# Score products of 32 rows in eight array tiles, and a second attention whose output has features on partitions

## The chip, the cores and the metric

One core of one Trainium2 chip runs the whole program. The metric is device time in microseconds (us) of one execution; lower is better. The core has a matrix engine (TensorE, PE in the profile, with its weight loads as PEld), three engines for elementwise work (VectorE as DVE, ScalarE as ACT, GpSimd as POOL) and a queue of transfers issued by SyncE (SP). Matrix products go to PSUM, a memory of eight banks of 512 fp32 columns on 128 partitions; everything else is in SBUF.

## The reference

The input `x` (128, 64, 384) and a mask `adj` (128, 64, 64) go through two attention layers. Every one of the 128 graphs has 64 nodes of 384 features.

```python
h = jnp.maximum(_layernorm(x), 0.0)
# layer 0, 12 heads of 32: additive scores
hv = einsum('bnd,ade->bane', h, W);  th = tanh(hv)
attn = leaky(src + swap(dst))            # src, dst: th times w_src, w_dst
attn = softmax(where(~adj, -999, attn))
feat = elu(attn @ hv + b);  gate = sigmoid(h @ H_w.T + H_b)
x = x + gate * feat + (1 - gate) * h
h = jnp.maximum(_layernorm(x), 0.0)
# layer 1, 6 heads of 64: q, k, v projections
probs = softmax(q @ k.T / 8 + where(adj, 0, -9e15))
x = x + (probs @ v).reshape(...) @ Wf + bf
```

## The kernel before

The tokens are cut into 16 groups of 512 (four tiles of 128 tokens, each tile two graphs of 64 nodes). The program of every engine is written out by hand as a sequence of passes `i = 0..16`: pass `i` does layer 0 of group `i` and layer 1 of group `j = i - 1`, so every pass but the first and the last holds both. Engines meet only through semaphores (`wait_ge`, `then_inc`). A table, `RING`, lists the PSUM banks in the order in which PE fills them; a job takes bank `place % 8`, and `take` makes PE wait until the job that used that bank eight places earlier has been read.

Products of the big weights are made in fp32r in three parts, high times high, low times high, high times low (`product`). For that ACT copies a transposed tile out of PSUM rounded to fp32r (the high part: `hT0h`, `hT1h`), and DVE subtracts it from the PSUM value (the low part: `hT0l`, `hT1l`). Everything else on PE is plain fp32; each such matmul of the program is two MATMUL records of the trace (a transpose is one).

PE's work in one pass, in order: the values of layer 0 and the gate (two times four products of nine matmuls), transposes of `th` and of the normalised layer-1 input (kept in `p1`), `wsd` products (source and destination scores), `project` for q and k with layer 0's score products `blocks` between them, `values1`, layer 1's scores, transposes of both layers' probabilities, `attend0` for four token tiles and `attend1` for two pairs of them, transposes of the next group's `h0` and of the second attention's output, and the last product with `Wf`.

`blocks(pair)` computes the additive scores of one pair of token tiles in eight matmuls of 32 rows, 64 output partitions and 384 columns: operands of token tile `t` stand on partitions 32t to 32t+31, results of graph `g` go to output partitions 64g to 64g+63. So each matmul uses one of eight tiles of 32 rows by 64 columns of the array, and a call uses four of them, each twice:

```python
for half_of in range(2):
    for t in (2 * pair, 2 * pair + 1):
        for g in range(2):
```

`attend1(pair)` has the transposed, not yet normalised probabilities as stationary operand and the values `V1` with a column of ones as moving operand; its output has tokens on partitions and the row sum as 65th column. DVE (`divide1`) takes the reciprocal of that column and multiplies, into `p1`; PE transposes `p1` again (12 transposes, the job `attn1_low`); ACT and DVE make the high and the low part for the product with `Wf`.

`V1` is filled from `v_tok` by four DMAs (`values1_spread`), `mask1` is the last operation on DVE before the division of the attention outputs, and `seeded banks` are banks into which ACT has written the gate's bias or the mask before PE adds to them (`put_bias`, `put_mask`); these are unchanged.

## Time and profile before

| | before |
|---|---|
| time, median of 3 runs | 1048.03 us (1046.15 to 1048.07) |
| profiled execution: its time, its span | 1046.33 us, 1044.4 us |
| PE busy | 968.0 us, 93% |
| DVE busy | 775.1 us, 74% |
| ACT busy | 630.1 us, 60% |
| POOL busy | 273.4 us, 26% |
| mean granted clock of TensorE | 0.982 |

The profile is one execution, recorded instruction by instruction. The page gives busy times and shares; the views of the trace give instructions in order of time (the timeline), what ended each wait, and the chain of work that ended last. All times are in us from the start of the span. The 1.9 us between span and time lie before the first and after the last instruction.

### The profile page before, as it was taken

What the parts mean: (1) busy time and instruction counts of PE and PEld (TensorE: products, weight loads), DVE (VectorE), ACT (ScalarE), POOL (GpSimd) and SP (SyncE); (2) the same over time, 40 slices, a digit from 0 to 9 for tenths busy, and PEclk for the clock granted to TensorE, in tenths of its full rate; (3) what the DMA queues carried; (4) which work ended last, traced back from release to release, by engine and by line L of the source; (5) the groups of instructions that cost most, each with busy time, mean ns of one, the idle gap of its engine ahead of it and who ended that gap; (6) DMA issues with size and microseconds to landing.
All of it is one profiled execution on the core that took longest, in us unless ns stands there. A gap on an engine that the chain in (4) does not pass through costs nothing.

```text
span 1044.4 us, 24816 instructions
## 1 busy us (share of the span) xinstructions
PE 968.0 (93%) x10037; PEld 840.1 (80%) x10037; DVE 775.1 (74%) x1456; ACT 630.1 (60%) x1242; POOL 273.4 (26%) x338
## 2 busy tenths in 40 slices
PE   6689999999999999999999999999999999999696
PEld 5487978889797888978788897878879788887575
DVE  4868877777787778868777886877788687877814
ACT  5657576484746757485675747567574755756332
POOL 2223150502415041240504124050421405032110
PEclk9699999999999999999999999999999999999987
DMA  8310151420415143041513405141240414121102
GB/s 233 51 24 11 32 93 32 91 33 32 62 33 93 32 81 44 16 78 33 93 32 74 49 4 92 32 93 32 68 48 11 94 32 93 33 49 23 23 31 62
DMA packets 183797, 56.61 MB, mean 54 GB/s; under 512 B 164994, under 2 KB 183684, under 8 KB 183684
## 3 DMA queue, kind: packets, MB, share of 16 engines
q1 hardware_dynamic: 183684, 55.02, 28.9%
q8 instruction: 81, 1.33, 0.5%
q14 instruction: 32, 0.26, 0.1%
HBM read 17.26 MB, written 12.58 MB: 29 GB/s over the span
## 4 chain that ended last, share of the span: by engine, by line
PE 53%; DVE 25%; issue 9%; ACT 6%; POOL 4%; DMA 1%; SPq 0%; DVEq 0%; ACTq 0%; POOLq 0%
PE ps L661 12%; PE ps L663 11%; PE ps L662 11%; PE ps L647 7%; PE ps L739 5%; PE ps L839 4%; DVE x L1001 4%; DVE ee L998 4%; DVE hT0l L907 3%; DVE hT1l L1096 3%; PE ps L857 3%; ACT p L440 2%; DVE p L1026 2%; DVE mx L1024 2%; PE ps L805 2%
## 5 line engine op out<-in xcount | busy, mean ns | idle before, releaser
L420 POOL TENSOR_TENSOR x_in<-x_in,ee 128x384 f32<-128x384 f32 x64 | 68.5, 1070 | 615.1 <-DVE ee L1004 615.1
L1060 DVE TENSOR_TENSOR hT1l<-ps,hT1h 128x512 fp32r<-128x512 f32 x48 | 30.4, 684 | 93.5 <-ACT hT1h L575 93.4
L647 PE MATMUL ps<-ident,p 128*128 128x128 f32 x576 | 80.4, 285 | 19.3 <-ACT p L440 10.7
L413 POOL TENSOR_TENSOR x_in<-x_in,h 128x384 f32<-128x384 f32 x64 | 85.1, 1359 | 16.4 <-DVE Wf_lo L932 16.4
L1037 DVE COPY_PREDICATED_SCALAR z<-not_adj,masked 128x768 f32 x64 | 69.6, 1087 | 26.3 <-ACT z L528 26.3
L647 PEld LDWEIGHTS ps<-ident,p 128*128 128x128 f32 x576 | 65.5, 145 | 28.1 <-issue 12.5
L661 PE MATMUL ps<-Wf_hi,hT1h 128*128 128x384 f32 x192 | 69.0, 359 | 10.4 <-DVE hT1l L1096 10.4
L491 ACT ACTIVATE ps<-hb_all 128x384 f32<-128x384 f32 x56 | 27.7, 495 | 79.6 <-DVE x_in L1049 79.6
L407 POOL TENSOR_TENSOR x_in<-x_in,bf_row 128x384 f32<-128x384 f32 x64 | 62.4, 1008 | 43.1 <-ACT p L440 43.1
L528 ACT ACTIVATE z<-ps 128x384 f32<-128x384 f32 x128 | 52.5, 498 | 30.9 <-PE ps L739 30.9
L661 PE MATMUL ps<-W_hi,hT0h 128*128 128x384 f32 x192 | 65.4, 341 | 3.5 <-DVE hT0l L907 3.5
L509 ACT ACTIVATE QT<-ps,bq_col 128x512 f32<-128x512 f32 x48 | 33.0, 687 | 58.1 <-PE ps L663 58.1
L1016 DVE TENSOR_TENSOR v_tok<-ps,bv_row 128x384 f32<-128x384 f32 x64 | 34.2, 553 | 44.9 <-PE ps L663 44.9
L891 DVE BATCH_NORM_STATS2 stats<-x_in 128x6 f32<-128x384 f32 x128 | 63.2, 543 | 5.4 <-DMA x_in<-in_x_dram 5.4
L661 PE MATMUL ps<-hT1h,Wq_hi 128*128 128x512 f32 x144 | 60.0, 416 | 6.6 <-DVE hT1l L1060 6.6
L663 PE MATMUL ps<-W_hi,hT0l 128*128 128x384 f32 x192 | 65.1, 339 | 0.0
L662 PE MATMUL ps<-W_lo,hT0h 128*128 128x384 f32 x192 | 65.1, 339 | 0.0
L663 PE MATMUL ps<-Wf_hi,hT1l 128*128 128x384 f32 x192 | 64.6, 336 | 0.0
L663 PE MATMUL ps<-Wv_hi,hT1l 128*128 128x384 f32 x192 | 64.5, 336 | 0.0
L663 PE MATMUL ps<-Hw_hi,hT0l 128*128 128x384 f32 x192 | 64.5, 336 | 0.0
L662 PE MATMUL ps<-Wf_lo,hT1h 128*128 128x384 f32 x192 | 64.5, 336 | 0.0
L661 PE MATMUL ps<-Hw_hi,hT0h 128*128 128x384 f32 x192 | 64.5, 336 | 0.0
(132 smaller groups left out, 2820.0 us busy)
## 6 DMA issues: line engine op xcount, KB each, us to landing
V<-v_tok SPq DMA_DIRECT2D x128, 192.0 KB, 4.9
x_in<-in_x_dram SPq DMA_DIRECT2D x16, 768.0 KB, 5.0
out_dram<-x_in SPq DMA_DIRECT2D x16, 768.0 KB, 3.5
x<-in_L_gnn_H_w_dram SPq DMA_DIRECT2D x1, 576.0 KB, 5.9
QT<-in_L_gnn_W_dram SPq DMA_DIRECT2D x3, 192.0 KB, 6.7
thT<-in_L_gnn_Wq_dram SPq DMA_DIRECT2D x1, 576.0 KB, 8.1
z<-in_L_gnn_Wk_dram SPq DMA_DIRECT2D x1, 576.0 KB, 8.6
z<-in_L_gnn_Wv_dram SPq DMA_DIRECT2D x1, 576.0 KB, 9.7
```

The source lines that it names most:

```text
L407: pool.tensor_tensor(x_in[:, j % 3, t], x_in[:, j % 3, t], bf_row[:], ALU.add).then_inc(x2_biased, 1)
L413: pool.tensor_tensor(x_in[:, i % 3, t], x_in[:, i % 3, t], h0[:, par, t], ALU.add).then_inc(x_plus_h, 1)
L420: pool.tensor_tensor(x_in[:, i % 3, t], x_in[:, i % 3, t], ee[:, t], ALU.subtract).then_inc(x2_made, 1)
L528: act.activation(z[:, t, half_of * D:(half_of + 1) * D], ps[:, job("leaky_made", 2 * t + half_of) % BANKS, 0:D], ACT.Prelu, alpha=SLOPE).t ...
L647: return pe.transpose(dst, src, ident[0:rows, 0:rows])
L661: pe.matmul(dst, left_h(c), right_h(c), start=(c == 0 and not begun), stop=False, skip_group_check=begun)
L662: pe.matmul(dst, left_h(c), right_l(c), start=False, stop=False, skip_group_check=begun)
L663: mm = pe.matmul(dst, left_l(c), right_h(c), start=False, stop=(c == C - 1 and not more), skip_group_check=begun)
L739: mm = pe.matmul(ps[64 * g:64 * g + 64, job("leaky_made", 2 * t + half_of) % BANKS, 0:D], src_rows[rows, g * N:(g + 1) * N], thT[rows].rea ...
L839: mm = pe.matmul(bank[g * N:(g + 1) * N, k], turned[:, at * P + g * N:at * P + (g + 1) * N], V0[:, g, :, t, k], start=True, stop=True, ski ...
L891: dve.bn_stats(stats[:, layer, t], src).then_inc((stats0, stats1)[layer], 1)
L1037: dve.copy_predicated(zt, not_adj[:, t].unsqueeze(1).broadcast_to((P, HEADS0, N)), masked0[:].unsqueeze(2).broadcast_to((P, HEADS0, N))).t ...
```

## The change

**Score products.** `blocks` is called with a half of the heads instead of a pair of token tiles. It covers all four token tiles, graph 0 first and then graph 1, so each call uses all eight array tiles once. `leaky`, the mask, the maximum, the subtraction and `exp0` follow: their units are (half of the heads, pair of token tiles), with as many elements as before.

**Second attention.** The probabilities are normalised in SBUF before they are transposed (`divide1(pair)`: a sum, a reciprocal and a multiplication over 768 elements per partition, two pairs). `attend1` has the values as stationary operand (64 keys x 64 features) and the transposed probabilities as moving operand (64 queries), so its output has features on partitions and is copied straight into `hT1h`/`hT1l`; the 12 transposes of the attention output and the column of ones are gone. Odd token tiles keep the heads of a pair swapped in `p1` (`p1_heads`), so one token tile's two heads come from both halves of the rows and go into one bank, and the other token tile's two heads use the other two of the four 64 x 64 array tiles. Four matmul records in a row use the same array tile. `V1` is filled by eight DMAs of half the size.

**Order.** Transposes are made and copied by token tile (four banks of 384 columns) instead of by chunk of 128 features (three banks of 512). `turn_h0` comes in two halves, `attend0(2)` and the first half of it now stand ahead of the transposes of layer 1's probabilities, `attend0(3)` stands ahead of `attend1`. `project` does all high-part products first and waits for the low parts after that. `attend1`'s second call takes banks that were used by the first two `h0_low` jobs, its first call banks of `attend0(1)` and `attend0(2)`.

```diff
+        def p1_pair(pair):
+            return p1[:, pair * P1_PAIR:(pair + 1) * P1_PAIR].rearrange("p (t x) -> p t x", t=2)[:, :, 0:D]
...
+        def p1_heads(pair, o):
+            pitch = P1_TILE + N if o == 0 else P1_TILE - N
+            at = pair * P1_PAIR + N * o
+            return p1[:, at:at + 2 * pitch].rearrange("p (t x) -> p t x", t=2)[:, :, 0:D]\
+                .rearrange("p t (k w) -> p t k w", w=P)[:, :, :, 0:N]
...
             + jobs("probs0T_copied", 0, probs0T_copied, 6)
-            + jobs("attn0_made", 0, attn0_made, 4)[0:2]
+            + jobs("attn0_made", 0, attn0_made, 4)[0:3]
+            + jobs("h0_low", NEXT, h0_low, 4)[0:2]
             + jobs("probs1T_copied", 1, probs1T_copied, 3)
-            + jobs("attn0_made", 0, attn0_made, 4)[2:3]
-            + jobs("attn1_made", 1, attn1_made, 4)
             + jobs("attn0_made", 0, attn0_made, 4)[3:4]
-            + jobs("h0_low", NEXT, h0_low, 3)
-            + jobs("attn1_low", 1, attn1_low, 3)
+            + jobs("attn1_low", 1, attn1_low, 4)
+            + jobs("h0_low", NEXT, h0_low, 4)[2:4]
             + jobs("out_made", 1, out_made, 4)
...
+                        for r in range(2):
+                            for b in range(2):
+                                sp.dma_start(V1[64 * r:64 * r + 64, g, b].rearrange("p q k e -> p (q k) e"),
+                                             v_tok[64 * g:64 * g + 64, 2 * b:2 * b + 2]
+                                             .rearrange("p q (k o e) -> p (q k) o e", o=2, e=E1)[:, :, r ^ b])\
...
+            def high_tile(to, name, t):
+                toks = slice(t * P, (t + 1) * P)
+                return act.activation(to[:, :, toks], ps[:, job(name, t) % BANKS, 0:D].rearrange("p (c m) -> p c m", m=P), ACT.Copy)
...
+                if real(i + 1):
+                    h0_parts(i + 1, range(0, 2))
                 if real(j):
                     for c in range(3):
                         act.wait_ge(probs1_turned, 3 * j + c + 1)
                         act.activation(KT[:, c], ps[:, job("probs1T_copied", c) % BANKS], ACT.Copy).then_inc(probs1T_copied, 1)
                 exp_elu(0)
                 exp_elu(1)
+                exp_elu(2)
...
-                    for c in range(C):
-                        act.wait_ge(attn1_turned, C * j + c + 1)
-                        act.activation(hT1h[:, c], ps[:, job("attn1_low", c) % BANKS], ACT.Copy).then_inc(attn1_high, 1)
+                    for t in range(TILES):
+                        act.wait_ge(attn1_full, 2 * j + t // 2 + 1)
+                        high_tile(hT1h, "attn1_low", t).then_inc(attn1_high, 1)
...
+            def turn_tokens(name, ready, done, src, i, g, tiles=range(TILES)):
+
+                for t in tiles:
+                    take(i, job(name, t))
+                    pe.wait_ge(ready, TILES * g + t + 1)
+                    for c in range(C):
+                        mm = turn(ps[:, job(name, t) % BANKS, c * P:(c + 1) * P], src(t, c))
                     mm.then_inc(done, 1)
...
+                    dst = ps[:, job(name, o) % BANKS]
+                    pe.wait_ge(h1_high, TILES * (j + 1))
+                    for c in range(C):
+                        pe.matmul(dst, wh[w][:, c, cols], hT1h[:, c], start=(c == 0), stop=False)
+                        pe.matmul(dst, wl[w][:, c, cols], hT1h[:, c], start=False, stop=False)
+                    pe.wait_ge(h1_low, TILES * (j + 1))
+                    for c in range(C):
+                        mm = pe.matmul(dst, wh[w][:, c, cols], hT1l[:, c], start=False, stop=(c == C - 1))
+                    mm.then_inc(full, 1)
...
-                def blocks(pair):
-                    take(i, job("leaky_made", 4 * pair + 3))
...
-                    for half_of in range(2):
-                        for t in (2 * pair, 2 * pair + 1):
...
                             rows = slice(SD * t, SD * t + SD)
-                            for g in range(2):
-                                mm = pe.matmul(ps[64 * g:64 * g + 64, job("leaky_made", 2 * t + half_of) % BANKS, 0:D],
...
+                def blocks(half_of):
+                    for t in range(TILES):
+                        take(i, job("leaky_made", 4 * half_of + t))
+                    for g in range(2):
+                        for t in range(TILES):
...
+                            mm = pe.matmul(ps[64 * g:64 * g + 64, job("leaky_made", 4 * half_of + t) % BANKS, 0:D],
+                                           src_rows[rows, g * N:(g + 1) * N],
+                                           thT[rows].rearrange("p c m -> p (c m)")[:, (2 * g + half_of) * D:(2 * g + half_of + 1) * D],
+                                           start=True, stop=True, skip_group_check=True)
...
-                        take(i, job("attn1_made", 2 * pair + o))
-                    for t in range(2):
-                        for k in range(PAIRS1):
...
+                    for k in range(PAIRS1):
+                        for b in range(2):
+                            t = 2 * pair + b
+                            q, at = divmod(t * PAIRS1 + k, 4)
                             for o in range(2):
-                                rows = slice(64 * o, 64 * o + 64)
-                                bank = ps[:, job("attn1_made", 2 * pair + o) % BANKS, 0:HEADS1 * (E1 + 1)]\
-                                    .rearrange("p (t k e) -> p t k e", t=2, e=E1 + 1)
+                                rows = slice(64 * (o ^ b), 64 * (o ^ b) + 64)
                                 for g in range(2):
-                                    mm = pe.matmul(bank[g * N:(g + 1) * N, t, k], KT[rows, q, at * P + g * N:at * P + (g + 1) * N],
-                                                   V1[rows, g, t + 2 * pair, k], start=True, stop=True, skip_group_check=True)
+                                    mm = pe.matmul(ps[64 * o:64 * o + 64, job("attn1_low", t) % BANKS, k * P + g * N:k * P + (g + 1) * N],
+                                                   V1[rows, g, b, pair, k], KT[rows, q, at * P + g * N:at * P + (g + 1) * N],
+                                                   start=True, stop=True, skip_group_check=True)
...
                 attend0(0)
                 attend0(1)
-                if real(j):
-                    turn_probs("probs1T_copied", probs1_made, probs1_turned, p1, PAIRS1, j, 3)
                 attend0(2)
+                if real(i + 1):
+                    turn_h0(i, i + 1, 1 - par, range(0, 2))
+                if real(j):
+                    turn_probs("probs1T_copied", probs1_divided, pair_of, probs1_turned, p1_tile, PAIRS1, j, 3)
+                attend0(3)
                 if real(j):
                     attend1(0)
                     attend1(1)
-                attend0(3)
                 if real(i + 1):
-                    turn_h0(i, i + 1, 1 - par)
-                if real(j):
-                    pe.wait_ge(attn1_made, TILES * (j + 1))
-                    turn_tokens("attn1_low", attn1_made, attn1_turned, lambda t, c: p1[:, t, c * P:(c + 1) * P], i, j)
+                    turn_h0(i, i + 1, 1 - par, range(2, 4))
+                if real(j):
...
+                        pe.wait_ge(attn1_low, TILES * j + t + 1)
...
-                        pair, o = divmod(q, 2)
-                        v = ps[:, job("attn1_made", q) % BANKS, 0:HEADS1 * (E1 + 1)].rearrange("p (t k e) -> p t k e", t=2, e=E1 + 1)
-                        sums = rs1[:, q].rearrange("p (t k) -> p t k", t=2)
-                        dve.wait_ge(attn1_full, 2 * j + pair + 1)
-                        dve.reciprocal(sums, v[:, :, :, E1]).then_inc(inv1_made, 1)
-                        dve.wait_ge(inv1_made, TILES * j + q + 1)
-                        dve.tensor_tensor(p1[:, 2 * pair:2 * pair + 2].rearrange("p t (k o e) -> p t k o e", o=2, e=E1)[:, :, :, o],
-                                          v[:, :, :, 0:E1], sums.unsqueeze(3).broadcast_to((P, 2, PAIRS1, E1)), ALU.mult)\
-                            .then_inc(attn1_made, 1)
+                        probs = p1_pair(pair).rearrange("p t (h m) -> p t h m", m=N)
+                        sums = rs1[:, 2 * pair:2 * pair + 2]
+                        dve.wait_ge(probs1_made, TILES * j + 2 * pair + 2)
+                        dve.tensor_reduce(sums, probs, AX_X, ALU.add).then_inc(sums1_made, 1)
+                        dve.wait_ge(sums1_made, 2 * j + pair + 1)
+                        dve.reciprocal(sums, sums).then_inc(inv1_made, 1)
+                        dve.wait_ge(inv1_made, 2 * j + pair + 1)
+                        dve.tensor_tensor(probs, probs, sums.unsqueeze(3).broadcast_to((P, 2, HEADS1, N)), ALU.mult)\
+                            .then_inc(probs1_divided, 1)
...
+                divide1(0)
+                divide1(1)
                 divide0(0)
                 divide0(1)
                 divide0(2)
-                if real(j):
-                    dve.wait_ge(probs1_turned, 3 * (j + 1))
-                for q in range(TILES):
-                    divide1(q)
-                if real(j):
-                    for c in range(C):
-                        dve.wait_ge(attn1_high, C * j + c + 1)
-                        dve.tensor_tensor(hT1l[:, c], ps[:, job("attn1_low", c) % BANKS], hT1h[:, c].bitcast(F32), ALU.subtract)\
-                            .then_inc(attn1_low, 1)
+                if real(i + 1):
+                    h0_lows(i + 1, range(0, 2))
+                if real(j):
+                    for t in range(TILES):
+                        dve.wait_ge(attn1_high, TILES * j + t + 1)
+                        low_tile(hT1l, hT1h, "attn1_low", t).then_inc(attn1_low, 1)
                 divide0(3)
                 if real(i + 1):
-                    h0_lows(i + 1)
+                    h0_lows(i + 1, range(2, 4))
```

PE, from layer 1's scores (`KT,QT`) on to the first matmuls of the `Wf` product; `ident` rows are transposes, of layer 0's probabilities `z`, of `p1` and of `h0`, `V,QT` and `V,thT` are `attend0`, `V,KT` is `attend1`. Before:

```order
L805 MATMUL ps<-KT,QT 64x64 x48
L647 MATMUL ps<-ident,z 128x128 x24
L839 MATMUL ps<-V,QT 64x66 x24
L647 MATMUL ps<-ident,p 128x128 x12
L839 MATMUL ps<-V,thT 64x66 x12
L857 MATMUL ps<-V,KT 64x65 x48
L839 MATMUL ps<-V,thT 64x66 x12
L647 MATMUL ps<-ident,h 128x128 x12
L647 MATMUL ps<-ident,p 128x128 x12
L661 MATMUL ps<-Wf_hi,hT1h 128x384
```

After:

```order
L828 MATMUL ps<-KT,QT 64x64 x48
L668 MATMUL ps<-ident,z 128x128 x24
L868 MATMUL ps<-V,QT 64x66 x24
L868 MATMUL ps<-V,thT 64x66 x12
L668 MATMUL ps<-ident,h 128x128 x6
L668 MATMUL ps<-ident,p 128x128 x12
L868 MATMUL ps<-V,thT 64x66 x12
L885 MATMUL ps<-KT,V 64x64 x48
L668 MATMUL ps<-ident,h 128x128 x6
L682 MATMUL ps<-Wf_hi,hT1h 128x384
```

`attend1` has moved behind `attend0(3)`, half of the `h` transposes have moved in front of those of `p`, and 12 of the 24 `p` transposes are gone.

DVE, from `mask1` on (`x` is `x1`, the output of `attend0`; `rs` are sums and reciprocals). Before:

```order
L1084 TENSOR_SCALAR mask<-adj_in 128x256
L977 RECIPROCAL rs<-ps 128x12
L979 TENSOR_TENSOR x<-ps,rs 128x384
L977 RECIPROCAL rs<-ps 128x12
L979 TENSOR_TENSOR x<-ps,rs 128x384
L977 RECIPROCAL rs<-ps 128x12
L979 TENSOR_TENSOR x<-ps,rs 128x384
L988 RECIPROCAL rs<-ps 128x6
L990 TENSOR_TENSOR p<-ps,rs 128x6x64
```

After:

```order
L1118 TENSOR_SCALAR mask<-adj_in 128x256
L1020 TENSOR_REDUCE rs<-p 128x12
L1022 RECIPROCAL rs<-rs 128x12
L1024 TENSOR_TENSOR p<-p,rs 128x2x384
L1020 TENSOR_REDUCE rs<-p 128x12
L1022 RECIPROCAL rs<-rs 128x12
L1024 TENSOR_TENSOR p<-p,rs 128x2x384
L1010 RECIPROCAL rs<-ps 128x12
L1012 TENSOR_TENSOR x<-ps,rs 128x384
L1010 RECIPROCAL rs<-ps 128x12
```

The division of layer 1 stood behind three divisions of `attend0`'s output and read PSUM; it now stands ahead of them and works on 768 elements in SBUF.

PE, the first product of `project` behind the `wsd` products, with the semaphores waited for. Before:

```order
L661 MATMUL ps<-hT1h,Wq_hi 128x512 [waits h1_low,gate_tanh]
L662 MATMUL ps<-hT1l,Wq_hi 128x512
L663 MATMUL ps<-hT1h,Wq_lo 128x512
L661 MATMUL ps<-hT1h,Wq_hi 128x512 [waits h1_low]
L662 MATMUL ps<-hT1l,Wq_hi 128x512
L663 MATMUL ps<-hT1h,Wq_lo 128x512
L661 MATMUL ps<-hT1h,Wq_hi 128x512 [waits h1_low]
```

After:

```order
L749 MATMUL ps<-hT1h,Wq_hi 128x512 [waits h1_high,thT_copied]
L750 MATMUL ps<-hT1h,Wq_lo 128x512
L749 MATMUL ps<-hT1h,Wq_hi 128x512
L750 MATMUL ps<-hT1h,Wq_lo 128x512
L749 MATMUL ps<-hT1h,Wq_hi 128x512
L750 MATMUL ps<-hT1h,Wq_lo 128x512
L753 MATMUL ps<-hT1l,Wq_hi 128x512 [waits h1_low]
L753 MATMUL ps<-hT1l,Wq_hi 128x512 x2
```

Each third matmul used the low part `hT1l`, chunk by chunk; now six matmuls use the high part alone, and the wait for the low part stands behind them.

## Rows read from the trace of the kernel before

**Rows 1.** The page: busy times, and granted clock of TensorE in 40 slices.

```profile
PE 968.0 (93%) x10037; PEld 840.1 (80%) x10037; DVE 775.1 (74%) x1456; ACT 630.1 (60%) x1242; POOL 273.4 (26%) x338
PEclk9699999999999999999999999999999999999987
```

**Rows 2.** DVE's `mask1`, one a pass: times, first and last start, form.

```profile
L1084 DVE TENSOR_SCALAR mask<-adj_in x16: 282/283/285, 52.3 to 967.8; 128x256 bf16<-128x256 uint8 x16
```

**Rows 3.** One pass by windows: length, busy time of each engine, PEclk, DMA.

```profile
538.00:599.20 61.20, 59.20 (x629) 51.79 (x626) 47.50 (x89) 38.96 (x77) 16.84 (x20) 1.00 0.35 53
```

**Rows 4.** Timeline of PE: start, length, line, count [idle before <-releaser].

```profile
570.40 0.86 PE L753 MATMUL ps<-thT,wsd 128*32 128x128 f32 x24 [0.62 <-ACT thT L569]
571.70 0.47 PE L661 MATMUL ps<-hT1h,Wq_hi 128*128 128x512 f32 x1 [0.44 <-DVE hT1l L1060]
576.07 1.52 PE L739 MATMUL ps<-thT,src_rows 32*64 32x384 f32 x16
577.52 0.51 PE L661 MATMUL ps<-hT1h,Wq_hi 128*128 128x512 f32 x1
...
602.62 1.74 PE L857 MATMUL ps<-V,KT 64*64 64x65 f32 x96
604.28 0.92 PE L839 MATMUL ps<-V,thT 128*64 128x66 f32 x24
605.13 1.53 PE L647 MATMUL ps<-ident,h 128*128 128x128 f32 x12
606.62 1.53 PE L647 MATMUL ps<-ident,p 128*128 128x128 f32 x12
608.84 0.42 PE L661 MATMUL ps<-Wf_hi,hT1h 128*128 128x384 f32 x1 [0.69 <-DVE hT1l L1096]
...
615.46 0.34 PE L661 MATMUL ps<-W_hi,hT0h 128*128 128x384 f32 x1
```

**Rows 5.** Timeline of PE inside the first `blocks` call, two narrow windows.

```profile
576.77 0.50 PE L739 MATMUL ps<-thT,src_rows 32*64 32x384 f32 x4
...
577.09 0.50 PE L739 MATMUL ps<-thT,src_rows 32*64 32x384 f32 x4
```

**Rows 6.** Timeline of DVE in the same pass.

```profile
579.83 0.95 DVE L1040 TENSOR_REDUCE mx<-z 128x12 f32<-128x768 f32 x1
580.82 0.96 DVE L1042 TENSOR_TENSOR z<-z,mx 128x768 f32<-128x768 f32 x1
581.69 1.09 DVE L1037 COPY_PREDICATED_SCALAR z<-not_adj,masked 128x768 f32 x1
...
599.43 0.23 DVE L977 RECIPROCAL rs<-ps 128x12 f32<-128x12 f32 x1
599.69 0.56 DVE L979 TENSOR_TENSOR x<-ps,rs 128x384 f32<-128x384 f32 x1
...
612.33 0.55 DVE L998 SCALAR_TENSOR_TENSOR ee<-ee,x 128x384 f32<-128x384 f32 x1
```

**Rows 7.** Timeline of ACT at the turn of a pass, and behind it.

```profile
566.02 2.51 ACT L440 ACTIVATE p<-x_in,shift,rstd 128x384 f32<-128x384 f32 x4 [0.21 <-POOL shift L389]
...
568.80 1.54 ACT L569 ACTIVATE thT<-ps 128x512 f32<-128x512 f32 x3
...
577.72 1.64 ACT L528 ACTIVATE z<-ps 128x384 f32<-128x384 f32 x4 [0.85 <-PE ps L739]
...
599.35 0.94 ACT L539 ACTIVATE p<-p 128x384 f32<-128x384 f32 x2
```

**Rows 8.** The chain that ended last, in order of time: start, length, what.

```profile
619.58 0.46 DVE x_in L1049
...
632.83 0.14 issue
```

**Rows 9.** Timeline of SP, the four DMAs that fill `V1`.

```profile
594.69 3.64 SPq L348 DMA_DIRECT2D V<-v_tok x4
```

**Rows 10.** The page on the same DMAs: count, KB each, median us to landing.

```profile
V<-v_tok SPq DMA_DIRECT2D x128, 192.0 KB, 4.9
```

198 lines of the change are left out of this document (95 added, 103 removed).

## The prediction

> **What bounds the kernel now.** I read the page first: PE is busy 93% of the span, DVE 74%, and TensorE's clock is granted in full in all slices but the first and the last [rows 1]. So I look at PE's own waits. `mask1` comes once a pass; from the first to the last of its 16 starts are 915.5 us, 61.0 us a pass [rows 2]. One undisturbed pass cut out as a window has PE busy for 59.20 of 61.20 us, DVE for 47.5, ACT for 39.0 [rows 3]: PE idles 2.0 us a pass. The timeline of PE says where: 0.62 us before the `wsd` products for ACT's copy, 0.44 us before `project` for DVE's low part, 0.69 us before the product with `Wf`, again for a low part [rows 4]. The rest are crumbs inside the `Wf` product: its 36 matmuls and their waits last from 608.84 to 615.46, 6.62 us [rows 4]. PE work that is removed therefore counts in full unless another engine's chain runs beside it. Two such chains lie near: DVE's from the divisions to the end of the pass, and ACT's at the turn of the pass, where `normalise1` waits only 0.21 us for POOL behind its own earlier work [rows 7].
>
> The profiled execution took 1046.33 us (span 1044.4 and 1.9 around it). The median of the runs shown is 1048.03, 1.7 more; the sum is made on 1046.33 and 1.7 is added. No change is told from about 0.2% (2 us) on.
>
> **Score products.** A call of `blocks` takes 1.45 us, from 576.07 to the next product at 577.52, for 16 records; there are two calls a pass [rows 4]. Inside it, records start in fours, and the fours are 0.32 us apart [rows 5]. Four record groups make 1.28 us, and 0.17 us are start and end of the call. 0.32 us is what 384 columns take at two clocks of 2.4 GHz each, so a group of four is four matmuls side by side in four array tiles, and an array tile is the thing that is occupied. In the old order each of four array tiles gets four records one after the other; in the new order each of eight gets two. If the eight run side by side, the call is 2 x 0.32 + 0.17 = 0.81 us, and with four more starts a few ns apart 0.83: 0.62 us less a call, 1.24 a pass, 16 passes: **19.8 us**. From the other side: if four is the most that run at once, 16 records are again four groups, and nothing is gained. The trace never shows more than four at once, but it shows both halves of what is needed, two column tiles on the same rows with different moving data and two row tiles on the same output partitions. I take eight. ACT's `leaky` and DVE's softmax behind it have the same element counts in other units: nothing.
>
> The Trainium skill, "TensorE: Matmul & The Clock Gate", Part 3, says that a pack of matmuls in separate array tiles lasts one matmul and about 4 ns for each tile more, and gives 10.6 times for 16 tiles. By it the call would be 0.64 us and its ends, the same sum as by the group distance; this trace agrees up to four tiles, and no row shows more.
>
> **Transposes of the second attention's output.** 12 go, 1.5 us of PE a pass (twelve alike last from 605.13 to 606.62) [rows 4]. They do not come back as such, because DVE's chain is what PE waits for there. I walk it on the clock of the shown pass, in which `mask1` ends at 599.43 and the score part's gain is left out.
>
> DVE's new `divide1(pair)` is a sum over 768 elements, a reciprocal and a multiplication: 0.99 + 0.26 + 0.87 us by the start-to-start times of the same shapes [rows 6]. Two pairs: 599.43 to 603.67. (Its inputs are in time: `exp1` of the second pair ends at 600.29 [rows 7].) Three divisions of `attend0` at 0.26 + 0.46: to 605.83 [rows 6, 8]. Two low parts of `h0` at 0.46: to 606.75. PE's `attend1` takes its banks from just these: its first call may start at 605.83 and its second at 606.75, each 0.13 later for the semaphore [rows 8], so the second starts at 606.88. Before, `attend1` started at 602.62. A call is half of the 1.66 us between 602.62 and 604.28 [rows 4]: to 607.71. Six transposes of `h`, half of 1.49: the `Wf` product can start at **608.46** instead of 608.84, 0.38 us earlier. Its low parts are there by then, since ACT and DVE need two copies and two subtractions of 0.4 to 0.5 us after the first call. Inside the product, the waits for chunks go, but its second tile's bank waits for the fourth division of `attend0`, which stands behind four low parts: about 0.2 us in place of 0.38. So layer 0's values start 0.56 us earlier than before.
>
> PE then holds no wait up to the gate's last products, and ACT's third gate tanh comes 0.56 earlier. `normalise1` behind it gains the 0.21 it had waited for POOL as well, if POOL is early enough [rows 7]. It is: DVE reaches `close(0)` at 612.33 before; after, four low parts end near 609.4, one division and two low parts later it is 611.1, 1.2 earlier, and DVE then runs without a wait to the statistics that POOL needs. So `normalise1` is 0.77 us earlier. Behind it two sets of three copies of 512 columns become two sets of four of 384: 1.64 instead of 1.54 us a set [rows 7], 0.2 lost for both by their lengths. `project` starts 0.57 us earlier. It now waits for ACT's high parts, and the low parts, 0.5 us behind, are covered by six matmuls of 0.23; without that cover it would cost 0.5. The 15 passes that have both layers: **8.6 us**.
>
> **Moved or added at nothing.** `attend1` itself keeps its 96 records of nearly the same size, 64 columns instead of 65. Each array tile gets four records in a row now, where neighbours used to differ; I take the old 1.66 us, because `blocks` also has two records of a matmul in a row on each array tile and still runs four side by side. Rivals below price that. `V1`'s DMAs: four issues take 3.64 us from 594.69 [rows 9] and a landing takes 4.9 us at the median [rows 10]. If each of the eight takes SP as long as one of the four, 0.91, the last is issued at 601.1 and lands at 606.0, just when `attend1` wants it at 605.96; with half as many packets each, it lands sooner. Cover is thus 0 to 3 us, and nothing is queued behind them on SP but the store of the output, which waits for much later work. The transposes of `p1` wait for DVE, up to 603.8, and `attend0(3)`, behind them, for the first division: PE idles there, but not for longer than the walk above holds it. The reordering of `h0_low` by tile takes no time from PE.
>
> **Sum.** 19.8 + 8.6 = 28.4: 1046.3 - 28.4 = 1017.9, plus 1.7: **1020 us**.
>
> **Rivals.**
>
> *Four at once is the most* (the score products' change does nothing). For it: no row with more. Against it: the tiles are separate in every row. Only the 8.6 us remain: 1048.0 - 8.6 = 1039. Chance 0.17.
>
> *`attend1` slows to two array tiles at a time.* Either because four records in a row for one array tile hold up the next, or because its two row halves write one bank. The nearest row with two array tiles is `attend0`, 24 records in 0.85 us from 604.28 to 605.13 [rows 4], so 96 take 3.4 us, 1.74 more, on DVE's and PE's path: 16 x 1.74 = 28 us, which gives 1048, no change. If the hold-up is only partial, from the group distance of 0.32 us for 384 columns a 64-column record takes 0.054 us, and 96 by two 2.6 us: 15 us, which gives 1035. Chance 0.17, a quarter of it at the upper end.
>
> The Trainium skill, "TensorEngine Tiling (Array Packing)", Restrictions and Gotchas, states that "Different row tiles cannot access same PSUM bank simultaneously". Before, `attend1` gave each row half its own bank; now both halves write each bank, on different partitions. By that rule this rival happens, in the first form. The trace has no place where two row tiles write one bank, so it neither agrees nor disagrees.
>
> *Slower: `attend1` with one array tile at a time.* 96 x 0.054 + 0.2 = 5.4 us, 3.7 more a pass, 60 us: 1080. It decides from `attend1` longer than 1.66 + 28.4/16 = 3.4 us on. For it: the same four records in a row. Against it: the group starts of `blocks`, where the second record of each array tile does not hold up the other array tiles. Chance 0.05.
>
> *Both of the first two*, or a late `V1` as well: 1055. Chance 0.04.
>
> **How the numbers follow.** The forecast has a chance of 0.57; its own range is 1010 to 1029: down to 1010 if PE gets back 0.6 us more of the 1.5 us of transposes a pass, up to 1029 if the walk along DVE gives nothing. The range for 8 in 10 takes in the first rival and the milder form of the second, 1010 to 1042. Faster by over 0.2%: 0.57 + 0.17 + 0.13 = 0.87. Within 0.2%: 0.04, the hard form of the second. Slower: 0.09.
>
> **What the profile after would show.** The `blocks` line: two calls a pass, each 0.8 us to the next product, windows inside it with eight records at once (four: first rival). The `attend1` line: 96 records in 1.7 us or less (3.4 or 5.4: second or third). PE idle a pass grows, from 2.0 to about 3.5 us, with waits for `probs1_divided`, `attn0_made` and `h0_low` in the attention part, while the pass is about 59.4 us by `mask1`. The `Wf` product starts some 9.0 us after `mask1` ends (9.4 before). The prediction is wrong if a DVE operation on the new layout costs more than its old shape, if `project` starts no earlier, or if the clock falls in the longer gaps.

## The result: 2.2% faster

The changed kernel takes 1023.87 us (median of 4 runs, 1023.79 to 1024.71), the kernel before 1047.09 us beside it (4 runs, 1045.91 to 1048.07). The ratio is 0.9777, with a 95% interval of 0.9764 to 0.9789. The profiled execution took 1024.71 us, 21.6 less than the one of before.

The page after: PE's and DVE's busy time and the granted clock in 40 slices, to be held against [rows 1].

```profile
PE 927.5 (91%) x9845; PEld 818.3 (80%) x9845; DVE 796.8 (78%) x1472; ACT 637.8 (62%) x1306; POOL 273.8 (27%) x337
PEclk9698999999999999999999999999999999999988
```

PE lost 40.5 us of work but the span only 21.5: PE now idles more. DVE has 22 us more to do. Where the 21.5 us lie is read from three windows: from the first `mask1` to the second, from there over 14 passes to the last, and to the end (columns: window, length, busy time of PE, PEld, DVE, ACT and POOL with instructions, granted clock, DMA). Before:

```profile
52.31:107.57 55.26, 51.54 (x509) 44.09 (x507) 41.30 (x74) 36.21 (x70) 17.17 (x20) 0.99 0.16 25
107.57:967.85 860.28, 830.31 (x8768) 724.09 (x8764) 663.68 (x1226) 543.34 (x1074) 234.44 (x276) 1.00 0.30 52
967.85:1044.40 76.55, 54.21 (x589) 46.53 (x586) 35.52 (x75) 20.71 (x37) 9.76 (x12) 0.86 0.14 35
```

After:

```profile
49.66:107.01 57.35, 54.05 (x512) 46.04 (x510) 41.48 (x76) 36.22 (x73) 17.22 (x20) 0.92 0.17 23
107.01:945.52 838.51, 793.59 (x8599) 703.56 (x8596) 682.64 (x1240) 550.49 (x1130) 234.79 (x276) 1.00 0.32 54
945.52:1022.90 77.38, 51.84 (x565) 44.87 (x562) 38.08 (x74) 21.11 (x40) 9.76 (x12) 0.86 0.16 38
```

The 14 middle passes give 21.8 us, 1.55 a pass. The ends give nothing: the first `mask1` is 2.65 us earlier, but the next window is 2.09 us longer, at a granted clock of 0.92 instead of 0.99, and the tail 0.83 us longer. In the middle PE idled 30.0 us of 860.3 before (2.1 a pass) and 44.9 of 838.5 after (3.2 a pass).

PE after, from the transposes behind the gate to the first `blocks` call (timeline; answers to [rows 4]); the last row is the same call cut off at 624.20:

```profile
615.95 1.47 PE L668 MATMUL ps<-ident,p 128*128 128x128 f32 x12
618.10 0.86 PE L776 MATMUL ps<-thT,wsd 128*32 128x128 f32 x24 [0.68 <-ACT thT L459]
619.72 0.47 PE L749 MATMUL ps<-hT1h,Wq_hi 128*128 128x512 f32 x1 [0.75 <-ACT hT1h L459]
...
624.09 0.90 PE L762 MATMUL ps<-thT,src_rows 32*64 32x384 f32 x16
624.92 0.50 PE L749 MATMUL ps<-hT1h,Wq_hi 128*128 128x512 f32 x1
...
624.09 0.58 PE L762 MATMUL ps<-thT,src_rows 32*64 32x384 f32 x8
```

Eight records now run at once, where four did [rows 5], and the call lasts 0.83 us to the next product instead of 1.45. Ahead of it stands a wait of 0.75 us for ACT's high parts `hT1h`, where 0.44 us for one low part stood.

PE after, second attention and start of the product with `Wf`:

```profile
592.97 1.96 PE L885 MATMUL ps<-KT,V 64*64 64x64 f32 x96 [0.54 <-DVE x L1012]
594.86 0.88 PE L668 MATMUL ps<-ident,h 128*128 128x128 f32 x6
595.49 0.42 PE L682 MATMUL ps<-Wf_hi,hT1h 128*128 128x384 f32 x1
...
596.96 0.34 PE L684 MATMUL ps<-Wf_hi,hT1l 128*128 128x384 f32 x1
597.36 0.45 PE L682 MATMUL ps<-Wf_hi,hT1h 128*128 128x384 f32 x1
597.64 0.34 PE L683 MATMUL ps<-Wf_lo,hT1h 128*128 128x384 f32 x1
...
602.16 0.34 PE L682 MATMUL ps<-W_hi,hT0h 128*128 128x384 f32 x1
```

And DVE in the same stretch (answers to [rows 6]):

```profile
586.11 0.28 DVE L1118 TENSOR_SCALAR mask<-adj_in 128x256 bf16<-128x256 uint8 x1
586.31 0.94 DVE L1020 TENSOR_REDUCE rs<-p 128x12 f32<-128x768 f32 x1
...
592.74 1.01 DVE L935 TENSOR_TENSOR hT0l<-ps,hT0h 128x384 fp32r<-128x384 f32 x2
594.62 1.95 DVE L935 TENSOR_TENSOR hT1l<-ps,hT1h 128x384 fp32r<-128x384 f32 x4 [0.87 <-ACT hT1h L459]
596.49 0.22 DVE L1010 RECIPROCAL rs<-ps 128x12 f32<-128x12 f32 x1
596.75 0.56 DVE L1012 TENSOR_TENSOR x<-ps,rs 128x384 f32<-128x384 f32 x1
```

DVE runs without a gap from `mask1` to 592.74, and `attend1` starts 0.23 us after the third division. Then DVE idles 0.87 us for ACT, and only behind four low parts comes the fourth division (596.49), for whose bank PE stops between 596.96 and 597.36.

### The profile page after: what moved, and what is told of

It reads as the page before. It is cut to its first block, busy times and chain, and to the rows that moved or that the text cites. A ratio compares the mean times of both kernels' runs of the same rounds, so it can differ in the third digit from the quotient of the medians.

```text
span 1022.9 us, 24747 instructions
## 1 busy us (share of the span) xinstructions
PE 927.5 (91%) x9845; PEld 818.3 (80%) x9845; DVE 796.8 (78%) x1472; ACT 637.8 (62%) x1306; POOL 273.8 (27%) x337
## 4 chain that ended last, share of the span: by engine, by line
PE 67%; DVE 23%; ACT 6%; issue 2%; POOL 1%; DMA 0%; ACTq 0%; POOLq 0%; DVEq 0%
PE ps L682 12%; PE ps L684 12%; PE ps L683 12%; PE ps L749 8%; PE ps L750 7%; PE ps L753 7%; PE ps L668 4%; DVE p L1059 3%; DVE x L1012 3%; DVE mx L1057 3%; DVE p L1024 3%; ACT hT1h L459 3%; PE ps L762 3%; DVE rs L1020 3%; DVE hT1l L935 3%
## 5 line engine op out<-in xcount | busy, mean ns | idle before, releaser
L935 DVE TENSOR_TENSOR hT1l<-ps,hT1h 128x384 fp32r<-128x384 f32 x128 | 62.7, 550 | 117.7 <-ACT hT1h L459 117.7
L668 PE MATMUL ps<-ident,p 128*128 128x128 f32 x384 | 54.3, 286 | 27.1 <-DVE p L1024 15.4
L668 PEld LDWEIGHTS ps<-ident,p 128*128 128x128 f32 x384 | 44.5, 145 | 32.6 <-issue 18.3
L503 ACT ACTIVATE gate<-ps 128x384 f32<-128x384 f32 x64 | 31.1, 486 | 54.9 <-PE ps L684 53.6
L682 PE MATMUL ps<-Wv_hi,hT1h 128*128 128x384 f32 x192 | 64.5, 336 | 0.0
```

The costliest lines, as they stand in the source:

```text
L668: return pe.transpose(dst, src, ident[0:rows, 0:rows])
L682: pe.matmul(dst, left_h(c), right_h(c), start=(c == 0 and not begun), stop=False, skip_group_check=begun)
L935: return dve.tensor_tensor(to[:, :, toks], ps[:, job(name, t) % BANKS, 0:D].rearrange("p (c m) -> p c m", m=P), high[:, :, toks].bitcast(F ...
```

## Experiments

Each ratio is against the kernel before on the same chip; its medians there lay between 1047.2 and 1047.6 us. "Steady pass" is the commonest distance between two `mask1` in the profiled execution.

**Do the two parts add up?** The kernel before with the score products and the units of the softmax behind them in the new form and nothing else; and the changed kernel with both in the old form. The edit of the first, at its head:

```diff
-                def blocks(pair):
+                def blocks(half_of):
```

> The kernel before with the score products alone in the new form (a half of the heads for all four token tiles, eight array tiles, and the units of the leaky step and the softmax behind it). My theory: a call of blocks goes from 1.45 to 0.83 us as in the changed kernel, nothing else changes, and because PE is what bounds the pass all of it counts: 2 x 0.62 x 16 = 19.8 us, so 1047.1 - 19.8 = 1027.3 us, mask1 to mask1 60.0 us instead of 61.26 in the steady passes. Rival (the gain needs the rest of the change, since in the kernel before ACT or DVE close up behind the scores): the call is 0.83 us but the pass gets less than 0.6 us shorter, so 1037 us or more. The passes of the kernel before that are up to 0.7 us longer than the others, because of a stop inside attend1, should still be there if the stop belongs to attend1's old form.

> The changed kernel with the score products and the softmax units of the kernel before. My theory: the two parts add up, so this loses 1.24 us a pass against the changed kernel: 1023.9 + 19.8 = 1043.7 us, steady pass 61.1 us. What is left to the second attention and the order is then 1047.1 - 1043.7 = 3.4 us, of which 0.13 us x 15 = 2 us are in the steady passes and the rest is the stop inside the old attend1 that is gone. The prediction's own figure for this part was 8.6 us, so 1038.5 us; it falls if this run is above 1041. Rival (the parts need each other): 1047 us or more.

Measured: 1027.73 us (1027.52 to 1028.74), ratio 0.9816 (0.9802 to 0.9829), steady pass 60.02; and 1042.24 us (1039.35 to 1042.95), ratio 0.9944 (0.9931 to 0.9957), steady pass 61.12. So the score products are worth 19.5 us added to one kernel and 18.4 us taken from the other: they are 1.24 us a pass on PE in either. The rest is worth 5.0 us. The 14 middle passes of the second run take

```profile
108.74:964.37 855.63, 810.81 (x8599) 711.09 (x8596) 682.00 (x1239) 550.68 (x1130) 234.43 (x276) 1.00 0.30 53
```

4.65 us less than before. Only 14 x 0.14 = 2 us of that is a shorter steady pass (61.26 to 61.12). The other 2.7 us are stops that came in many passes of before, as in this one:

```profile
356.88 1.28 PE L857 MATMUL ps<-V,KT 64*64 64x65 f32 x68
358.81 0.68 PE L857 MATMUL ps<-V,KT 64*64 64x65 f32 x28 [0.65 <-issue]
```

Of the 2.6 us by which the middle passes of before exceed 14 steady ones, 2.1 us lie in passes with such a stop in `attend1`, and 0.6 us in three passes whose `attend1` ran undisturbed, in 1.58 us, and which lost their time elsewhere. The stops are still there in the run with the score products alone (middle passes 60.02 to 60.50) and nearly gone in the two kernels with the new `attend1`. "issue" means that the profile shows nothing PE waited for. Six of the later kernels with the new `attend1` had one or two middle passes that a stop of this kind made 0.3 to 0.8 us longer, so the old form makes them frequent but isn't needed for one. What they are stays open.

**What made `attend1` longer?** Rotated order; and a bank for each row half, for which the odd heads of the two token tiles of a pair change places, so that this kernel computes another output from operations of the same sizes:

```diff
                     for k in range(PAIRS1):
-                        for b in range(2):
+                        for g in range(2):
+                            for b in range(2):
...
-                                for g in range(2):
```

```diff
-            pe.matmul(ps[64 * o:64 * o + 64, job("attn1_low", t) % BANKS, ...
+            pe.matmul(ps[64 * o:64 * o + 64, job("attn1_low", 2 * pair + (o ^ b)) % BANKS, ...
```

> The changed kernel with attend1's loops in another order, so that each of four matmuls in a row has another of the four 64 x 64 array tiles (two records in a row on an array tile instead of four); banks, operands and counts are the same. Theory of the runs (in the changed kernel the records stand one behind the other for their array tile, which costs about 0.04 us in each of six steps): attend1 goes from 1.89 back to 1.66 us, the pass from 59.88 to 59.66, and the time to 1023.9 - 3.4 = 1020.5 us. Theory of the shared bank (both row halves write one bank): nothing changes, 1.89 us and 1023.9 us. If DVE is what the product with Wf waits for anyway, attend1 is 1.66 us long and the time stays at 1023.9.

> The changed kernel with attend1 in its order, but each row half of the array writes a bank of its own (the odd heads of the two token tiles of a pair change places, so the output is another one; sizes and counts are unchanged). Theory of the shared bank: attend1 goes from 1.89 to 1.66 us, 1020.5 us. Theory of the runs: 1.89 us stays, 1023.9 us. If both count, each of this run and the one with the rotated order gives a part of the 0.22 us.

Measured: 1020.38 us (1019.69 to 1024.22), ratio 0.9751 (0.9736 to 0.9767), and 1024.36 us (1023.78 to 1024.65), ratio 0.9780 (0.9766 to 0.9793). The timelines, rotated order first, then own banks:

```profile
532.58 1.86 PE L885 MATMUL ps<-KT,V 64*64 64x64 f32 x96 [0.54 <-DVE x L1012]
534.36 0.87 PE L668 MATMUL ps<-ident,h 128*128 128x128 f32 x6
```

```profile
533.25 1.96 PE L885 MATMUL ps<-KT,V 64*64 64x64 f32 x96 [0.54 <-DVE x L1012]
535.14 0.33 PE L668 MATMUL ps<-ident,h 128*128 128x128 f32 x1
```

With own banks `attend1` is exactly as long as with shared ones, 1.89 us: the shared bank costs nothing. With the rotated order it is 1.78 us (532.58 to 534.36), and the pass is 59.79 instead of 59.88 us. So four records in a row for one array tile cost 0.1 us a pass, half of the 0.22 that I had put down to them. The 0.22 is itself too little: the 1.66 us of the pass shown before hold a short stop, and where nothing disturbed it the old `attend1` took 1.58. Most of the rest is between the calls: the second one starts 0.93 us after the first in either order (0.75 before), since it takes the bank of DVE's second `hT0l`. The 48 records of the first call start within 0.71 us before and in the rotated order, and within 0.81 us with four in a row; the wait for the bank covers that 0.1. By the trace the edit is worth 1.1 us (middle passes 837.45 us in place of 838.51); the median is 3.5 us lower, but its highest run, the profiled one, isn't, and I do not count that difference.

**What does `project` wait for?** First, the layer-1 input transposed and copied by chunk as before, and `project` as before, each chunk's three matmuls behind that chunk's low part. Second, the same transposes and copies, but `project` with the high parts first, and its waits by chunk; against the changed kernel this edit of `project` is:

```diff
-                    pe.wait_ge(h1_high, TILES * (j + 1))
                     for c in range(C):
+                        pe.wait_ge(h1_high, C * j + c + 1)
                         pe.matmul(dst, wh[w][:, c, cols], hT1h[:, c], start=(c == 0), stop=False)
                         pe.matmul(dst, wl[w][:, c, cols], hT1h[:, c], start=False, stop=False)
-                    pe.wait_ge(h1_low, TILES * (j + 1))
                     for c in range(C):
+                        pe.wait_ge(h1_low, C * j + c + 1)
```

> The changed kernel with the layer-1 input transposed and copied as before (three banks of 512 columns, by chunk of features), and project as before: each chunk's three matmuls wait for that chunk's low part. th stays by token tile. Theory (the last step of my 8.6 us failed here: project now waits for all four of ACT's high copies, 0.75 us, where it waited 0.44 us for one high and one low part): normalise1 to project goes from 6.05 us back to about 5.7, 0.35 a pass, 15 passes: 1023.9 - 5.3 = 1018.6 us. Rival (the four shorter copies are themselves what costs, not what project waits for; th has four of them as well): less than half of it comes back, 1021.5 us or more.

> As the run with the layer-1 input by chunk, but project keeps the new order (six matmuls with high parts first, then the three with low parts) and waits chunk by chunk, first for high parts, then for low parts. Theory: the first chunk's copy ends during the wsd products, so the wait of 0.75 us before project goes altogether, and the lows (0.5 us behind) lie under six matmuls of 0.23: 0.75 x 15 = 11.2 us, 1012.7 us. Rival (the wait only moves inside, to the second or third chunk's copy): as the run with the order of before, about 1018.6 us.

Measured: 1019.45 us (1018.29 to 1020.06), ratio 0.9732 (0.9718 to 0.9745), steady pass 59.57; and 1013.17 us (1011.46 to 1014.70), ratio 0.9670 (0.9656 to 0.9684), steady pass 59.09. Both as the theory had it. With high parts first the wait is gone (PE, then ACT):

```profile
728.64 0.86 PE L783 MATMUL ps<-thT,wsd 128*32 128x128 f32 x24 [0.68 <-ACT thT L460]
729.43 0.50 PE L756 MATMUL ps<-hT1h,Wq_hi 128*128 128x512 f32 x1
...
728.45 1.59 ACT L595 ACTIVATE hT1h<-ps 128x512 fp32r<-128x512 f32 x3
```

PE starts `project` at 729.43 while ACT still copies chunks two and three. A token tile's copy is worth nothing to `project`, which needs all tokens of a chunk; a chunk's copy is worth two matmuls.

**The bank of the fourth division, and all three together:**

```diff
                     h0_lows(i + 1, range(0, 2))
+                divide0(3)
                 if real(j):
...
-                divide0(3)
```

> The changed kernel with one operation moved on DVE: the fourth division of attend0's output (0.72 us for both instructions) stands ahead of the four low parts of attn1 instead of behind them. PE has made its input before attend1 starts, and DVE idles 0.87 us there for ACT's first high part. Theory: the second tile of the product with Wf no longer waits for the bank (0.23 us in the trace), so Wf's product goes from 6.66 to about 6.4 us, 15 passes: 1020.5 us. Rival (the low parts of attn1 are what PE waits for): the division pushes them back and the product starts later, 1024 us or more.

> The changed kernel with three edits together: attend1's matmuls rotated over the array tiles (0.1 us a pass by its trace), the layer-1 input by chunk with high parts first (0.75 expected), the fourth division of attend0 ahead of the low parts (0.23 expected). If they add up: 1.08 us a pass, 15 passes, 16.2 us less than 1023.9: 1007.7 us. Rival (something else closes up, for example DVE's low parts of the layer-1 input behind its longer tail): at most the best single one, 1012 us or more.

Measured: 1018.03 us (1016.17 to 1018.91), ratio 0.9717 (0.9704 to 0.9730), steady pass 59.55; and 1005.67 us (1004.03 to 1007.54), ratio 0.9602 (0.9589 to 0.9615), steady pass 58.64. The stop in the product is gone:

```profile
713.94 0.34 PE L684 MATMUL ps<-Wf_hi,hT1l 128*128 128x384 f32 x1
714.11 0.34 PE L682 MATMUL ps<-Wf_hi,hT1h 128*128 128x384 f32 x1
```

It was worth 0.33 us a pass, not 0.23: after a stop the first matmul took 0.28 us to the next (597.36 to 597.64), against 0.17 in a row. Together the three edits (rotated order, chunks with high parts first, earlier division) give 59.88 - 58.64 = 1.24 us; one by one they give 0.09, 0.79 and 0.33, so they add up.

**Is DVE's chain the bound up to `attend1`?** Here DVE sums 16 of the 64 keys and adds 1 in place of the reciprocal; the probabilities are scaled wrongly by it, and nothing else changes:

```diff
-                        dve.tensor_reduce(sums, probs, AX_X, ALU.add).then_inc(sums1_made, 1)
+                        dve.tensor_reduce(sums, probs[:, :, :, 0:16], AX_X, ALU.add).then_inc(sums1_made, 1)
...
-                        dve.reciprocal(sums, sums).then_inc(inv1_made, 1)
+                        dve.tensor_scalar(sums, sums, 1.0, None, ALU.add).then_inc(inv1_made, 1)
```

> The changed kernel with DVE's two sums of the second attention over 16 of the 64 keys only, and an addition of 1 in place of the reciprocal behind them (same size), so the probabilities are scaled otherwise; everything else is unchanged. It asks whether DVE's chain from mask1 on is what attend1 waits for. From 0.98 us for 768 elements and 0.26 for 12 (start to start) a sum over 192 elements is about 0.4 us: DVE's chain is 1.15 us shorter a pass. My theory (DVE's chain decides): attend1 starts 5.75 instead of 6.86 us after mask1, and nearly all of it counts: PE loses its waits of 0.55 us (second six transposes of p) and 0.54 us (attend1), 1.1 us x 15 = 16.5: 1007.5 us. Rival (ACT closes up, with its copies of the turned probabilities and three exponentials ahead of the first high part; or PE's own work does): less than 0.5 us a pass, 1016.5 us or more.

Measured: 1005.00 us (1002.93 to 1005.55), ratio 0.9592 (0.9579 to 0.9605), steady pass 58.77.

```profile
579.10 1.47 PE L668 MATMUL ps<-ident,p 128*128 128x128 f32 x12
580.50 0.92 PE L868 MATMUL ps<-V,thT 128*64 128x66 f32 x24
581.45 1.96 PE L885 MATMUL ps<-KT,V 64*64 64x64 f32 x96
```

`attend1` starts 5.55 us after `mask1`, PE runs without a wait up to it, and 1.11 us of the pass are gone. DVE's chain was the bound, until PE's own work took over, and its two sums of 0.98 us each are a price that the new form pays on it.

**Order of the eight.**

```diff
-                    for g in range(2):
-                        for t in range(TILES):
+                    for t in range(TILES):
+                        for g in range(2):
```

> The changed kernel with the eight matmuls of a call of blocks in another order: token tile after token tile, the two graphs of one directly behind each other (they share their 32 rows), instead of all four token tiles of one graph first. Theory (what is occupied is the array tile, and each of the eight gets one matmul in either order): the call stays at 0.83 us, 1023.9 us. Rival (two column tiles on the same rows wait for each other when they are neighbours): a call of up to 1.45 us again, so up to 1043.7 us.

Measured: 1023.55 us (1023.16 to 1024.63), ratio 0.9771 (0.9758 to 0.9784); the call still takes 0.84 us:

```profile
623.66 0.90 PE L762 MATMUL ps<-thT,src_rows 32*64 32x384 f32 x16
624.50 0.50 PE L749 MATMUL ps<-hT1h,Wq_hi 128*128 128x512 f32 x1
```

**Can POOL take a part of the sums?** Two tries on top of the three edits; the second folds only the second pair, and leaves the division where it was:

```diff
+                            pool.tensor_tensor(ee[:, pair] ..., probs[:, :, :, 0:N // 2], probs[:, :, :, N // 2:N], ALU.add)\
+                                .then_inc(folded1, 1)
...
-                        dve.tensor_reduce(sums, probs, AX_X, ALU.add).then_inc(sums1_made, 1)
+                        dve.wait_ge(folded1, 2 * j + pair + 1)
+                        dve.tensor_reduce(sums, ee[:, pair] ..., AX_X, ALU.add).then_inc(sums1_made, 1)
...
+                divide0(0)
                 divide1(0)
                 divide1(1)
-                divide0(0)
```

> The run with the three edits together, and POOL, which idles from mask1 on for over 10 us, takes half of DVE's two sums: it adds the two halves of each row (768 to 384 elements, one operation a pair, into a buffer that is free there), DVE sums 384 elements instead of 768, and the first division of attend0 stands ahead of both pairs so that POOL has time. Theory (DVE's chain decides up to attend1, as the run with the short sums showed): a sum of 384 is 0.46 us shorter (from 0.98 for 768 and 0.26 for 12), two of them 0.92 us; PE's own work from the transposes of p on leaves about 0.85 of it: 0.85 x 15 = 12.8 us less than 1005.7, 993 us, and attend1 starts 6.0 us after mask1. Rival (POOL's operation of 1.0 to 1.4 us comes too late for the first pair, or DVE and POOL slow each other while both work on SBUF): attend1 starts at 6.5 us or later and the time is 1000 us or more.

> The run with the three edits together, and only the second pair's probabilities folded by POOL (768 to 384 elements); the division of attend0 stays behind both pairs. In the run with two folds POOL's first operation ran beside DVE's mask1 and mask1 took 0.72 us to the next instruction instead of 0.20; the second fold ran beside DVE's fp32 operations, and they kept their lengths. Theory (the clash is with mask1 alone, and the moved division cost the rest): POOL now starts after the second pair's exponential, 1.2 us after mask1, mask1 keeps 0.2 us, DVE's chain is 0.46 us shorter, attend1 starts 6.40 instead of 6.86 us after mask1: 0.46 x 15 = 6.9 us less than 1005.7, 998.8 us. Rival (POOL's operation slows DVE's other ones here, or the fold comes too late): attend1 at 6.7 us or later, 1003 us or more.

Measured: 1004.01 us (1003.58 to 1005.47), ratio 0.9591 (0.9578 to 0.9605), steady pass 58.57, a time which cannot be told from the three edits alone; and 1008.01 us (1005.79 to 1010.06), ratio 0.9621 (0.9607 to 0.9636), steady pass 58.87, by the pass 0.23 us slower than without the fold (the intervals of the two ratios touch). Both of my theories missed; the rivals beside them named what came. `attend1` starts 6.67 and 7.08 us after `mask1`, 6.86 without a fold. Two folds, DVE and POOL:

```profile
691.12 0.80 DVE L1136 TENSOR_SCALAR mask<-adj_in 128x256 bf16<-128x256 uint8 x1
691.84 0.22 DVE L1026 RECIPROCAL rs<-ps 128x12 f32<-128x12 f32 x1
...
690.77 1.00 POOL L438 TENSOR_TENSOR ee<-p 128x384 f32<-128x384 f32 x1 [17.34 <-ACT p L568]
```

One fold, DVE and POOL:

```profile
695.62 1.58 DVE L1044 TENSOR_TENSOR p<-p,rs 128x768 f32<-128x768 f32 x1
697.12 0.54 DVE L1040 TENSOR_REDUCE rs<-ee 128x12 f32<-128x384 f32 x1
...
695.38 1.01 POOL L437 TENSOR_TENSOR ee<-p 128x384 f32<-128x384 f32 x1 [18.88 <-DVE rs L1040]
```

While POOL works, `mask1` takes 0.72 us to the next instruction instead of 0.20, and the multiplication of `p` 1.50 instead of 0.87. The extra 0.52 and 0.63 us are close to what was left of POOL's operation when each began (0.65 and 0.77), as if DVE stood still until POOL was done. POOL's second fold in the first of these runs ran beside a multiplication from PSUM and a sum, and these kept 0.48 and 0.57 us. So my theory that only `mask1` clashes was wrong: an operation with two SBUF operands clashes too. In the run with two folds, moreover, the moved division pushed the second pair back, and PE's transposes and `attend0(3)` behind it then set the start of `attend1`.

The Trainium skill, "SBUF — State Buffer", Who interferes with whom, says that a DVE instruction with two SBUF inputs contends with a GpSimd instruction that reads SBUF, that some forms of `tensor_scalar` do, that `tensor_reduce` doesn't on trn2, and that the one that comes second stands still for the whole of the other. By that rule each of the two operations loses what is left of POOL's, and sums lose nothing; these traces agree, within 0.14 us.

## Why the forecast held, and what was off in it

The forecast was 1020 us, the measurement 1023.87. The mechanism was right; 28.4 us were expected, and the profiled execution gave 21.6.

**Score products, 19.8 us: right.** 0.62 us a call and 1.24 a pass are what the trace shows, 19.5 and 18.4 us what the two runs show. Eight array tiles run side by side in either order, so the first rival is out. Their records start 6 to 7 ns apart, as the four of before did, and not the 4 ns that the prediction let stand as agreeing with its trace; on a call that is a few hundredths of a us. The clock did not give any of it back in the middle passes.

**Second attention and order, 8.6 us: mis-sized.** The sum was 0.57 us for a pass, and the steady passes show 0.14. The terms, read in one pass, add up to 0.12:

- *`Wf` product 0.38 us earlier, measured 0.23.* The walk along DVE's chain was good: the second `attend1` call was put 7.45 us behind `mask1`'s end and started 7.59 behind it (592.97 + 0.93 - 586.31). The difference is mostly between DVE's division and PE, 0.23 us where the row that the prediction took it from has 0.14. Then the call took 0.96 us in place of 0.83, of which the rotated order gives back 0.1, and the six transposes 0.63 in place of 0.75.
- *Waits inside the product 0.2 in place of 0.38, measured 0.05 lost.* The product takes 6.67 us (595.49 to 602.16), 6.62 before. The bank wait that I had named is the one; it costs 0.33 with what follows it, as the moved division shows.
- *`normalise1` gains 0.21 from POOL: it gained 0.3.* From layer 0's values to `normalise1` it was 11.82 us, now 11.51 (602.16 to 613.67).
- *The longer copies lose 0.2: `project` lost 0.37 behind `normalise1` (6.05 us, 5.68 before).* The copies themselves lost 0.1 (eight in 2.96 us, six in 2.86). The rest is the step that was wrong in kind. I had written that only the low parts matter and lie under six matmuls. But the wait had moved to the fourth high copy, 0.75 us, where PE had needed the first of three. The two runs by chunk show 0.31 and 0.79 us a pass.

That is 0.43 us less in each of the 14 middle passes, 6.0 us. The ends, for which the same terms gave 3.0 us, gave -0.3. In this stretch of the first passes, before and after, PE's idle time grew and its clock fell:

```profile
70.00:80.00 10.00, 8.33 (x73) 7.17 (x71) 3.70 (x13) 7.37 (x15) 5.57 (x9) 1.00 0.54 79
```

```profile
70.00:80.00 10.00, 6.84 (x54) 4.66 (x53) 3.73 (x13) 8.13 (x19) 6.24 (x9) 0.80 0.66 79
```

A granted 0.80 is a mixture of the two levels of 2.4 and 1.2 GHz. Two earlier runs say where this comes from: the window from the first `mask1` to the second is 55.18 us with the score products alone and 57.23 with them undone, so its 2 us belong to the second attention and its order. And with the layer-1 input by chunk they are gone:

```profile
50.33:105.37 55.04, 52.30 (x512) 44.97 (x510) 41.40 (x75) 36.15 (x72) 17.22 (x20) 0.96 0.18 24
```

From 70 to 90 us the granted clock is 1.00 before, 0.83 in the changed kernel and 0.91 by chunk, but 0.91 also with the score products undone, whose window is long: the clock alone isn't it. These are single executions, and no run took clock or waits away alone, so how the 3.3 us divide between them stays open. In the other direction, 2.4 us came from the stops of before, for which the prediction had no term (2.6 us there, 0.2 in the changed kernel). 28.4 - 6.0 - 3.3 + 2.4 = 21.5, the change of the span.

**`attend1` at its old 1.66 us: off by 0.2, and by 0.3 from the undisturbed 1.58.** The hold-up by four records in a row exists, but at 0.1 us a pass and not at 1 or 1.7. The bank that both row halves write costs nothing. The Trainium skill, "TensorEngine Tiling (Array Packing)", Restrictions and Gotchas, says that different row tiles cannot access the same bank at once. These runs do not bear that out as a price: two row halves wrote one bank on different partitions, 96 records in 1.89 us, and 1.89 us with a bank each; and in the rotated order with the shared bank the first call's 48 records start within the 0.71 us that they took before, when each half had its own.

**`V1`'s DMAs at nothing: right.** They landed by about 590.1 (eight issues from 581.57 in 6.10 us, and 2.4 us to the landing), 2.9 us before `attend1`. The page, on the landing:

```profile
V<-v_tok SPq DMA_DIRECT2D x128, 96.0 KB, 2.4
```

**Of what the profile after should show**, eight records at once, calls of 0.8 us and the clock in the steady passes came true; `attend1` in 1.7 us and a pass of 59.4 us did not (1.89, and 59.88); PE's idle time is 3.2 us a pass where I had said 3.5. The `Wf` product starts 9.18 us after `mask1` ends, where 9.0 was forecast. Of the signs of being wrong, DVE's new operations kept the times of their old shapes, `project` starts only 0.12 us earlier in the pass where 0.57 was forecast, and the clock fell in the first passes alone.

## What to carry to other kernels

When work is cut along another axis, look at which pieces its consumer can start with: cutting the layer-1 copies by token tile made PE wait for the last of four, and going back to chunks, with high parts first, gave 0.79 us a pass, where the second attention with its order had given 0.14. Small matmuls are counted by what their array tile carries: the same 16 records on twice the tiles took 0.83 us in place of 1.45, and order mattered only where one tile got four records in a row. A bank's last reader belongs ahead of the work that waits for another engine. With these three edits the kernel takes 1005.67 us, 4.0% less than before.

## What was not expected of the hardware

- An idle POOL is not free help for DVE: one POOL operation of 1.0 us lengthened DVE's `mask1` by 0.52 us and its multiplication of two SBUF operands by 0.63 us, but not its sums or its operations on PSUM.
- A stop of PE for a bank inside the `Wf` product (fp32r, 384 columns) cost 0.11 us more than its length: the first matmul after it took 0.28 us to the next instead of 0.17, in each of the 15 passes that have both layers.
- Stops of up to 0.8 us inside a row of small matmuls, which the profile puts down to nothing, lengthened `attend1` by 0.2 us or more in 7 and 10 of the 14 middle passes of the two kernels with its old form, and in none to two with the new one; passes with them hold 2.1 of the 4.65 us that this part of the change gained there.
